# Two expert stages in one block, over three chunks of groups

## What is computed

```
expert step 1:  e = exp(logits - max);  the 2 largest of 8 experts per token;  w = e / sum(e)
                y = sum over the 2 experts of  w * (relu(relu(x W1[e] + b1[e]) W2[e] + b2[e]) W3[e] + b3[e])      128 -> 256 -> 256 -> 128
expert step 2:  logits = y Wgate^T, again the 2 largest of 8 with softmax weights
                out = x1 + sum over the 2 experts of  w * (gelu(y W1[e] + b1[e]) W2[e] + b2[e])                     128 -> 512 -> 128
```

## Time and profile before

| | us |
|---|---|
| median of 3 runs | 2091.97 (2087.68 to 2100.49) |
| the profiled execution, its own time | 2083.64 |
| span in the profile | 2081.6 |
| first tile result to last, first stage | 310.3 to 453.6 |
| first tile result to last, second stage | 578.0 to 722.9 |
| first instruction of the field stage (SP's queue) | 755.78 |

### The profile page before, as it was taken

The page is one execution under the profiler, slowest core; times in us unless marked ns, Lnnn a source line. Parts: engine busy times, 40 slices in busy tenths (PEclk is TensorE's granted clock), DMA queues, the critical chain, the costliest instruction groups (busy, mean ns, idle before and its releaser), DMA issues. The chain is left out here.

```text
span 2081.6 us, 37284 instructions
## 1 busy us (share of the span) xinstructions
PE 1736.5 (83%) x12051; PEld 1241.9 (60%) x12051; DVE 1258.1 (60%) x3243; ACT 1067.8 (51%) x3158; POOL 873.5 (42%) x1095
## 2 busy tenths in 40 slices
PE   0899629974299849999868999999999999899887
PEld 0344429864198826556557677777777777555533
DVE  7587624536345378787667566655665665456556
ACT  0443204331143328788544566656666666666643
POOL 0246646546555513343318756070606060622233
PEclk9997659995599959999979999999999999999999
DMA  2920023322122250000023221212121212110001
GB/s 63 416 69 22 30 72 107 97 85 84 49 70 63 58 195 23 26 25 25 25 77 80 60 57 47 57 47 57 47 58 46 57 48 60 53 48 29 25 12 41
DMA packets 155838, 135.89 MB, mean 65 GB/s; under 512 B 87957, under 2 KB 128214, under 8 KB 153494
## 3 DMA queue, kind: packets, MB, share of 16 engines
q1 hardware_dynamic: 146582, 115.08, 18.9%
q0 software_dynamic: 9088, 18.70, 2.8%
HBM read 77.17 MB, written 56.54 MB: 64 GB/s over the span
## 5 line engine op out<-in xcount | busy, mean ns | idle before, releaser
L2676 DVE TENSOR_TENSOR delta_sv<-delta_sv,delta_zp 32x256 f32<-32x256 f32 x384 | 161.2, 420 | 168.4 <-PE delta_zp L2317 162.0
L818 POOL DMA_INDIRECT y<-moe_y,moe_aim x156 | 177.1, 1135 | 161.4 <-DVE moe_y L958 69.0
L2589 POOL TENSOR_TENSOR delta_dd<-delta_ll,delta_minus 128x1024 f32<-128x1024 f32 (+1 forms) x9 | 24.3, 2700 | 382.4 <-DMA delta_ll<-lanes 382.3
L1771 ACT ACTIVATE field_p<-field_sp,field_nm 128x128 f32<-128x128 f32 x512 | 179.9, 408 | 0.9 <-DVE field_nm L1855 0.8
L2596 POOL TENSOR_TENSOR delta_dd<-delta_dd,delta_prod 128x30 f32<-128x30 f32 (+11 forms) x270 | 151.4, 561 | 21.1
L2594 POOL TENSOR_TENSOR delta_prod<-delta_ll,delta_dd 128x30 f32<-128x30 f32 (+11 forms) x270 | 139.4, 516 | 21.2
L2317 PE MATMUL delta_zp<-delta_sv,delta_ct 128*32 128x128 f32 x1536 | 122.5, 281 | 20.1 <-DVE delta_sv L2676 12.4
L2285 PE MATMUL delta_xp<-delta_la,delta_di 128*128 128x256 f32 x512 | 121.4, 392 | 12.9 <-DMA delta_di<-inverses 7.0
L1771 ACT ACTIVATION_READ_ACCUMULATOR field_p<-field_sp,field_nm 128x1 f32 x512 | 127.6, 249 | 0.0
L2317 PEld LDWEIGHTS delta_zp<-delta_sv,delta_ct 128*32 128x32 f32 x1536 | 70.3, 110 | 85.0 <-DVE delta_sv L2676 50.7
L2285 PEld LDWEIGHTS delta_xp<-delta_la,delta_di 128*128 128x128 f32 x512 | 97.3, 194 | 37.6 <-issue 25.3
(11 more groups left out here) (564 smaller groups left out, 4554.3 us busy)
## 6 DMA issues: line engine op xcount, KB each, us to landing
delta_al<-alpha SPq DMA_DIRECT2D x33, 512.0 KB, 4.4
pairs<-c_none SPq DMA_DIRECT2D x16, 1032.0 KB, 16.3
moe_xg<-pairs SPq DMA_DIRECT2D x78, 129.0 KB, 2.2
moe_yt<-y SPq DMA_DIRECT2D x16, 512.0 KB, 4.5
w_E<-in_E_dram SPq DMA_DIRECT2D x1, 4624.0 KB, 36.9
w_E<-in_E_dram SPq DMA_DIRECT2D x8, 578.0 KB, 4.0
lanes<-delta_la SPq DMA_DIRECT2D x128, 32.0 KB, 1.7
delta_di<-inverses SPq DMA_DIRECT2D x64, 64.0 KB, 2.3
```

Of the source, the lines that this page charges most:

```text
L818: nc.gpsimd.indirect_dma_start(results, bass.IndirectOffsetOnAxis(ap=aim[:, t % AR, j:j + 1], axis=0), y[:, t % YS, j, :], None).then_inc( ...
L1771: last = nc.scalar.activation(p[:, slot, h, :], s_ps[i][:, k, :], ACT.Exp, bias=nm[:, slot, h:h + 1], accum_out=zs[:, slot, h:h + 1])
L2676: nc.vector.tensor_tensor(sv[rows, two, :], sv[rows, two, :], z_ps[2 * pair // HH][rows, at, :], ALU.subtract).then_inc(s["z_kept"], 1)
```

## The change

All 8 groups are split into three **chunks**: groups 0 to 2, 3 to 5, 6 and 7. Each chunk has its own region per expert, its own tiles and its own result array. A chunk of 3 groups has 12 full tiles and 7 more, 19; the last has 8 + 7 = 15. So `TILES` becomes 19 + 19 + 15 = 53 for each of the two layers.

Both layers' tiles run in one block (`experts`), 106 steps in all. Results of a tile are stored in order by SP with one direct DMA. When a chunk's tiles are stored, POOL fetches the rows of its groups with 8 indirect DMAs per group (`fetch`), and the combination of a group is cut into pieces that stand at the ends of fixed steps: at step r of `ROUTE_AT` ACT weighs the first result; at r+1 DVE adds (`mix`) and PE transposes; at r+2 ACT copies and PE computes logits; at r+3 DVE and ACT make the exponentials; at r+4 DVE picks and PE counts; at r+5 DVE places, and at a chunk's last group makes the tables; at r+6 the pair weights of a finished chunk. `FINISH_AT` does the same for the second layer, and its last two groups come after all tiles. Only the first 4 groups are scattered within retention; POOL scatters the other 4 at the start of the new block. The tables of chunk 0 are made within retention's loop. The pieces of `field_basis` stand at steps 2 to 17. The transposed tile and the result of a tile now have one PSUM bank each instead of two. The number of the pair and the aim are gone; a row has 512 bytes.

```diff
 
 CAP = B * T
 SLOTS = 256
-TILES = 2 * B * T // SLOTS + NE - 1
-ROW = D + 1
+SUBS = SLOTS // 128
+CHUNKS = ((0, 3), (3, 6), (6, 8))
+CHUNK_TILES = [(last - first) * GT * 2 // SLOTS + NE - 1 for first, last in CHUNKS]
+TILE0 = [sum(CHUNK_TILES[:k]) for k in range(len(CHUNKS) + 1)]
+TILES = TILE0[-1]
 PR = 4
 FILLS = 16
 PACKED = 1156
...
+def chunk_end(nc, ch, g, w, c, n):
+
+    ends = [last for _, last in CHUNKS]
+    if n + 1 not in ends:
+        return None
+    k = ends.index(n + 1)
+    ch.link(nc.vector.tensor_tensor(c["cnt"][:, k, :], g["behind"][:], w["region"][:, k, :], ALU.subtract))
+    if k + 1 < len(CHUNKS):
+        ch.link(nc.vector.tensor_copy(g["behind"][:], w["region"][:, k + 1, :]))
+    return k
...
+def tile_tables(nc, ch, g, w, c, layer, k):
+
+
+    n = CHUNK_TILES[k]
+    shape = [128, n, NE]
...
+ROUTE_AT = {128: (40, 45, 51, 72, 78, 83, 105, 111), 256: (24, 28, 32, 43, 47, 51, 59, 63)}[SLOTS]
+FINISH_AT = {128: (127, 133, 138, 156, 161, 167), 256: (77, 80, 83, 96, 99, 102)}[SLOTS]
...
+                for t in range(XR):
+                    load(t)
+                for t in range(2 * TILES):
+                    store(t)
+                    if t + XR < 2 * TILES:
+                        load(t + XR)
+                    if t < NE:
+                        sp.dma_start(w["E2"][:, t, :], E2[:, t, :]).then_inc(loaded_2, 16)
...
+                for u in range(PR, GROUPS):
+                    for b in range(GB):
+                        scatter(nc, pool, c, dram, u, b)
+                nc.gpsimd.memset(none[:], 0.0).then_inc(primed, 1)
+                for k, (first, last) in enumerate(CHUNKS):
+                    all_stored(0, k)
+                    pool.wait_ge(aimed, k + 1)
+                    for u in range(first, last):
+                        fetch(u, 0, k)
+                    for u in range(first, last):
+                        pool.wait_ge(g["placed"], u + 1)
+                        for b in range(GB):
+                            scatter(nc, pool, c, dram, u, b)
+                for k, (first, last) in enumerate(CHUNKS):
+                    all_stored(1, k)
+                    pool.wait_ge(aimed, len(CHUNKS) + k + 1)
+                    for u in range(first, last):
+                        fetch(GROUPS + u, 1, k)
...
+                def turn_rows(q):
+                    pe.wait_ge(mixed, q + 1)
+                    pe.wait_ge(turn_kept, q)
+                    for b in range(GB):
+                        last = nc.tensor.transpose(turn_ps[:, b * T:(b + 1) * T], c["rows"][:, q % PR, b, :], w["ident"][:])
+                    last.then_inc(rows_turned, 1)
+
+                def logits(u):
+                    pe.wait_ge(turn_kept, u + 1)
+                    if u >= 1:
+                        pe.wait_ge(g["placed"], u)
+                    for b in range(GB):
+                        last = nc.tensor.matmul(logit_ps[:, b * NE:(b + 1) * NE], mT[:, u % 2, b * T:(b + 1) * T], w["wg2"][:], start=True, stop=True)
+                    last.then_inc(g["logits"], 1)
+
+                def combine(step):
+                    for u in due(ROUTE_AT, step - 1):
+                        turn_rows(u)
+                    for u in due(ROUTE_AT, step - 2):
+                        logits(u)
+                    for u in due(ROUTE_AT, step - 4):
+                        gate_count(nc, pe, g, w, u, count_ps)
+                    for u in due(FINISH_AT, step - 1):
+                        turn_rows(GROUPS + u)
+
+                for s in range(-3, TILES):
+                    if s + 3 < TILES:
+                        turn(s + 3)
+                    if 0 <= s + 2 < TILES:
+                        first_layer(s + 2)
+                    if 0 <= s + 1 < TILES:
+                        second_layer(s + 1)
+                    if 0 <= s:
+                        third_layer(s)
+                        field_tensor(pe, s)
+                        combine(s)
...
+                def weigh(q):
+                    act.wait_ge(fetched[q % YR], 2 * GB * 16 * (q // YR + 1))
+                    for b in range(GB):
+                        first = yt[:, q % YR, b, 0, :]
+                        at = q % GROUPS * GB + b
+                        last = nc.scalar.activation(first, first, ACT.Identity, scale=c["weight"][:, 0, at:at + 1])
+                    last.then_inc(weighed, 1)
...
+                def keep_y(t):
+                    if t >= YS:
+                        dve.wait_ge(stored[t % YS], 16 * (t // YS))
+                    dve.wait_ge(y_made, t + 1)
+                    nc.vector.tensor_tensor(y[:, t % YS, :, :], y_ps, part(t, 1028).unsqueeze(1).to_broadcast([128, SUBS, D]),
+                                            ALU.add).then_inc(y_kept, 1)
+
+                def mix(q):
+                    dve.wait_ge(c["scattered"][q % PR], 2 * GB * 16 * min(2 + q // PR, 4))
+                    if q >= PR:
+                        dve.wait_ge(rows_turned, q - PR + 1)
+                    dve.wait_ge(weighed, q + 1)
+                    for b in range(GB):
+                        at = q % GROUPS * GB + b
+                        last = nc.vector.scalar_tensor_tensor(c["rows"][:, q % PR, b, :], yt[:, q % YR, b, 1, :], c["weight"][:, 1, at:at + 1],
+                                                              yt[:, q % YR, b, 0, :], ALU.mult, ALU.add)
+                    last.then_inc(mixed, 1)
...
+                def combine(step):
+                    for u in due(ROUTE_AT, step - 1):
+                        mix(u)
+                    for u in due(ROUTE_AT, step - 3):
+                        shift(u)
+                    for u in due(ROUTE_AT, step - 4):
+                        gate_pick(nc, dve, ch, g, c, u)
+                    for u in due(ROUTE_AT, step - 5):
+                        gate_place(nc, dve, ch, g, c, u, count_ps)
+                        k = chunk_end(nc, ch, g, w, c, u)
+                        if k is not None:
+                            tile_tables(nc, ch, g, w, c, 1, k).then_inc(tabled, 1)
+                            dve.wait_ge(tabled, len(CHUNKS) + k)
+                    for u in due(ROUTE_AT, step - 6):
+                        for k, (_, last) in enumerate(CHUNKS):
+                            if u + 1 == last:
+                                pair_weights(nc, ch, c, one, total, k).then_inc(aimed, 1)
+                    for u in due(FINISH_AT, step - 1):
+                        mix(GROUPS + u)
+                    for u in due(FINISH_AT, step - 2):
+                        residual(u)
+
+                gate_prime(nc, ch, g, w)
+                for s in range(-4, TILES):
+                    if s + 4 < TILES:
+                        stage_weights(s + 4)
+                    if 0 <= s + 3 < TILES:
+                        keep_x(s + 3)
+                    if 0 <= s:
+                        keep_y(s)
+                        for k in range(1, len(CHUNKS)):
+                            if s == 2 * k - 1:
+                                tile_tables(nc, ch, g, w, c, 0, k).then_inc(tabled, 1)
+                                dve.wait_ge(tabled, k)
+                        for k in range(len(CHUNKS)):
+                            if s == 7 + 2 * k:
+                                pair_weights(nc, ch, c, one, total, k).then_inc(aimed, 1)
+                        field_vector(dve, s)
+                        combine(s)
```

More of the change, by code:

```diff
@@ new lines, in third_layer @@
+                def third_layer(t):
+                    pe.wait_ge(h2_kept, H1 * (t + 1))
+                    if t >= 1:
+                        pe.wait_ge(y_kept, t)
+                    for j in range(SUBS):
+                        for k in range(H1):
+                            last = nc.tensor.matmul(y_ps[:, j, :], hid[:, t % 2, H1 + k, j * 128:(j + 1) * 128], part(t, 768 + k * 128),
+                                                    start=(k == 0), stop=(k == H1 - 1))
+                    last.then_inc(y_made, 1)
@@ new lines, in wide_layer @@
+                def wide_layer(t):
+                    pe.wait_ge(x_kept, t + 1)
+                    pe.wait_ge(staged, t + 1)
+                    n = t - TILES
+                    if n < 2:
+                        pe.wait_ge(h1_kept, H1 * TILES)
+                        pe.wait_ge(h2_kept, H1 * TILES)
+                    for i in range(H2):
+                        if n >= 2:
+                            pe.wait_ge(h_kept, H2 * (n - 2) + i // 2 * 2 + 2)
+                        nc.tensor.matmul(hidden(t % 2 * 2 + i // 2, i % 2), part(t, i * 128), xT[:, t % 2, :], start=True, stop=True).then_inc(h_made, 1)
@@ new lines, in last_layer @@
+                def last_layer(t):
+                    pe.wait_ge(y_kept, t)
+                    for j in range(SUBS):
+                        for k in range(H2):
+                            if j == 0:
+                                pe.wait_ge(h_kept, H2 * (t - TILES) + k + 1)
```

(14 more changed lines are left out.)

888 lines of the change are left out of this document (320 added, 568 removed).

## The result

The changed kernel took 2305.36 us (median of 4 runs, 2299.63 to 2315.01) against 2090.16 for the kernel before beside it (4 runs, 2087.68 to 2100.49): a ratio of 1.1024, 95% interval 1.0966 to 1.1082. It is slower, as forecast, but by 215 us where the forecast had 72, and far outside the range of 2115 to 2200.

A forecast was written before the change was run, and what follows sets the result against it. PE was taken to bound the tile stages, a chain over four engines the gap between them. Terms -30 - 117 - 13 + 0 + 104 + 20 + 74 + 34 = +72 on 2083.64 gave 2156; forecast 2160, range 2115 to 2200.

The forecast's parts named there:

- (4): Tail from the last result to the field stage: 32.5 us against 32.9 before, so 0 (-5 to +10).
- (11): POOL's queue: the fetch of group 6 stands behind group 5's scatters, so PE waits 6 us instead of 1.6, +5.
- rival C: POOL is the next bound: a fetch costs twice a scatter, 2.5 us, giving 2215; chance 0.08.
- (1): Start of the block: waits for DVE alone, first load at 267 instead of 297.02, -30 (-24 to -32).
- (2): Gap of 124.4 us between the stages becomes a pipeline fill of 7 between two layers, -117.
- (3): `pair_weights` as it was: its step took 9.99 us instead of 3.70; twice 6.3 saved, -13.
- (5): 28 more tiles on PE: 14 x 3.70 + 14 x 3.73 = +104 us.
- (6): The combinations' own matmuls on PE (logits 0.9, counts 0.5, four transposes about 0.5), hidden nowhere now, +20 us.
- (9): PE's `gate_count` waits for DVE's `gate_pick`: 2.2 us, 8 times, 18 us.
- (7): PE's `turn_rows` waits for DVE's `mix`: 1.6 us, 14 times, 22 us.
- (10): DVE-only pieces delay the next step's copies: PE waits 4.3 us at three chunk ends (13), about 2 us elsewhere.
- The clock: PE's clock falls behind waits: 5 x 3 = 15, and half of 13 waits of about 2 us, 19.5; +34 (15 to 54).

The follow-up runs named there:

- the control: The changed kernel run again, not a letter changed, on chip 10: 2164.86 us, ratio 1.0399 to the kernel before.
- chip 13: Changed kernel with PE's pieces one step later, run with bare waits (2262.91 us) and with a fill behind every two DMAs (2167.43); kernel before 2097.12.
- v1: Changed kernel, fills behind every four DMAs, PE's pieces one step later, next chunk's first fetch earlier, second layer's first tiles prepared in first layer's last steps: 2100.65 us.
- e10: Changed kernel with one fill behind every two indirect DMAs and PE's pieces one step later: 2118.76 us on chip 10, 2167.43 on chip 13.
- e7: Changed kernel with one fill of a small buffer behind every two indirect DMAs of the block: 2161.57 us, then 2169.26 beside the control.
- e13: Kernel before with a satisfied wait ahead of each pair of the 64 scatters between its two tile stages: 2088.38 us.
- e6: Kernel before with one more indirect DMA per tile for 30 tiles of the second tile stage: 2085.99 us.
- e3: Changed kernel with four POOL fills of a small buffer in place of each left-out indirect DMA of the block: 2169.02 us.

## Why the prediction was wrong, and where it was right

**The step that failed** is the overlap of POOL's runs with the tiles. It is no term of the sum but the reason why one was missing. I costed POOL's runs of indirect DMAs only by their own length, as work beside the others' (terms 4 and 11), and put rival C aside because "the engine only writes addresses in both directions". In the profile of the changed kernel the tiles stop inside every run of 24 to 32 of them: six runs, 140 us in all against the control. That POOL's issuing has a part in it was shown on chip 13 (95 us); for the chip of the measurement it rests on the same picture in the trace. Rival C had POOL as the culprit but by the wrong mechanism: a fetch is issued every 1.25 us, as a scatter is, and doesn't cost twice as much. Could it have been seen? The trace of before has no "remote" wait in its 64 scatters, probably since it was taken on a chip of the other kind: its own time, 2083.64, agrees with the chips without the hold-up (2080.7 to 2084.4), while the runs beside the changed kernel (2087.68 to 2100.49) tend to those with it (2096.6, 2097.1). I noted that difference of 8 us and explained it by nothing.

**The terms**, read from the control, where the hold-up is absent, against my sum (2156 on the profiled execution of before; the control's own profiled execution took 2160.05):

(1) The first load comes at 274.0 here and 269.2 in the first profile, forecast 267 of 297.0: -23 and -28 for -30. My 3 us from DVE's end to the load were 2.3 both times; but DVE ended at 271.7 and 266.9 where I had taken 264.3, so this term moves by 5 us from run to run. (2) From the last result of the first layer to the first of the second are 14.3 us, forecast 7: -110 for -117. What I had not counted is that the second layer's weights and rows are prepared only when the first layer's loop is through; `v1` moves them and gets 6.4. (3) My "twice 6.3" was read in the first stage alone. In the second the two steps around `pair_weights` take 7.24 and 5.45 in place of twice 3.73, 5.2 us more, so the term is nearer -11.5. (4) From the last result to the field stage: 826.10 - 794.3 = 31.8, forecast 32.5, before 32.9; SP's queue in the control:

```profile
826.10 0.83 SPq L1389 DMA_DIRECT2D field_xT<-x2T  x2
```

(5) Steps without a piece are 3.70 and 3.73 as forecast. (6) to (9), PE's pieces in the control with the waits ahead of them:

```profile
397.40 0.65 PE L1104 MATMUL moe_bank<-w_ident,c_rows 128*128 128x128 f32 x4 [1.63 <-DVE c_rows L1244]
397.89 0.38 PE L1047 MATMUL moe_bank<-w_ident,moe_xg 128*128 128x128 f32 x2
...
402.33 1.06 PE L1112 MATMUL moe_bank<-w_wg,moe_mT 128*128 128x8 f32 x8 [0.57 <-ACT moe_mT L1181]
...
412.88 0.41 PE L144 MATMUL moe_bank<-moe_kept,w_ones 128*128 128x32 f32 x2 [2.03 <-DVE moe_kept L136]
```

1.63 for my 1.6, 0.57 for 0.85, 2.03 for 2.2. The four transposes take 0.49 from their start to the next tile's, forecast 0.5; by the same measure the logits take 0.92 for 0.9 and the counts 0.47 for 0.5. `e10`, with the pieces a step later, shows that these waits were real and could be had back: 2161.57 - 2118.76 = 42.8, where (7) to (9) and their share of the clock were my 44 and up. These are single runs, and `e7` took 2169.26 beside the control, so the 43 are good to some 8 us. (10) PE's wait behind the tables of a chunk end:

```profile
471.64 0.66 PE L1047 MATMUL moe_bank<-w_ident,moe_xg 128*128 128x128 f32 x2 [4.42 <-DVE moe_xT L1228]
```

4.42 for my 4.3; behind the other two chunk ends it is 4.40 and 3.89. (11) The late fetch of group 6:

```profile
593.98 1.12 PE L1104 MATMUL moe_bank<-w_ident,c_rows 128*128 128x128 f32 x4 [6.14 <-DVE c_rows L1244]
```

6.14 for my 6. Both waits and their numbers were right.

**The clock.** I let half of the waits of 2 us cost 3.0 more. The control has both outcomes for nearly the same wait. Behind 2.03 us (412.88) the clock stays at 1.00 and the step takes 6.40; behind 2.00 us (434.33) it falls, and the step takes 8.05:

```profile
434.33 0.41 PE L144 MATMUL moe_bank<-moe_kept,w_ones 128*128 128x32 f32 x2 [2.00 <-DVE moe_kept L136]
```
```profile
413.00:414.00 1.00, 1.00 (x8) 0.97 (x9) 0.64 (x1) 0.00 (x0) 0.00 (x0) 1.00 0.28 80
435.00:436.00 1.00, 1.00 (x5) 0.82 (x4) 0.90 (x2) 0.00 (x0) 0.00 (x0) 0.59 0.50 130
436.00:437.00 1.00, 1.00 (x3) 0.78 (x3) 0.00 (x0) 0.08 (x1) 0.00 (x0) 0.50 0.06 18
```

So half was right for the counts, but a fall costs 8.05 - 6.40 = 1.65 and not 3.0. Of the five early waits that I had put at 2.0 one fell. It has a twin of the same length that kept the clock; their steps take 5.92 and 4.23:

```profile
325.21 0.41 PE L1047 MATMUL moe_bank<-w_ident,moe_xg 128*128 128x128 f32 x2 [2.76 <-DVE moe_xT L1228]
...
337.25 0.41 PE L1047 MATMUL moe_bank<-w_ident,moe_xg 128*128 128x128 f32 x2 [2.76 <-DVE moe_xT L1228]
```

So the length of the wait alone doesn't decide it; what does is not shown. Five falls at 1.65 are 8 us where I had 19.5. The Trainium skill (TensorE: Matmul & The Clock Gate, Why this matters for your kernels) warns only against longer gaps between bursts; the trace does not bear that out here, where four of the seven counts inside the layers lose the clock (steps of 8.03 to 8.05 us) and three keep it (6.40).

All in all the mechanism of the forecast is confirmed where the hold-up is absent: from the first to the last result 506.9 us where my terms give 412.6 - 117 - 13 + 104 + 20 + 74 + 34 = 514.6, the end of the block at 826.1 for 828, and 82 us more than the kernel before beside it (2164.86 - 2082.92) for my 72. That the end of the block is so close is in part luck. The start and the change of layers each came out 7 us longer than forecast, and the steps inside the two layers 15 us too short (506.9 - 14.3 = 492.6 for 507.6), most of which is the clock. Direction and sum were right for one kind of chip; the measurement was made on the other.

## What to carry to other kernels

Run the unedited kernel beside every cure, on the same chip: here three "cures" of one set gave the same time as no cure, and only the control showed it. When the profiled execution and the timed runs of one kernel differ by more than they scatter, ask whether they come from the same chip before costing anything. And a long unbroken run of POOL's indirect DMAs next to a pipeline of short tiles is a risk that no trace from a good chip shows: break it up. A fill behind every two DMAs cost 4 us where there was no hold-up (2169.26 against 2164.86) and gave back 95 where there was. And give engines that wait for each other one step of slack, which was worth about 43 us here.

## What the hardware showed that I had not expected

On some chips, counts that PE and DVE raise take effect late while POOL issues indirect DMAs back to back; DVE waited up to 26.6 us for one. An ACT count reached PE at once in the stretch shown (289.86 to 289.91); whether ACT's are spared everywhere is not shown. In that stretch ACT got its input at 296.09 and DVE, which waits for the eight matmuls behind it, at 306.57, though PE's record has both done by 286.94. The hold-up reached the changed kernel in six places (140 us) and the kernel before, with waits added (`e13`), in the stage between its tiles (12 us more there than in the first profile). On the three other chips (11, 10 and 0; before: 2080.7 to 2084.4) no trace has a "remote" wait in this part of the kernel, although POOL's runs are as long: 32 in the control, over 90 in `e6`. What in the chip does this stays open: the runs tell that POOL's issuing goes with it and that a gap of 0.3 us behind every two DMAs weakens it, not whether the path of the counts, POOL's writing of the descriptors or something else is what is shared. That POOL's fills alone do no harm (`e3`) was only tried on a chip where the DMAs would probably have done none either. The Trainium skill (DMA: Bandwidth & Descriptors, SWDGE vs HWDGE vs iDMA) tells of an interference in the other direction: VectorE, in its 2-port perf mode, keeps GpSimd out of the memory into which GpSimd writes descriptors. Here POOL went on at its even pitch and the others waited, so that rule doesn't cover it.
